# Five incidence rows of a graph layer turned by DMA, eleven by TensorE; the adjacency turned by DMA, its two halves added by GpSimd

## What is computed

```
L0: gt = adj.T;  x += (d^-.5 * gt * d^-.5) @ (h @ W0) + b0      d = row sums of gt
L1: mask = adj > 0;  inc = adj + mask / sqrt(row count of mask)
    x += (inc @ h) / row sums of inc
L2: ht = h @ W (4 heads of 256);  e = leaky_relu(src_i + dst_j) + adj
    x += mean over heads of softmax(e) @ ht
L3: x += relu(adj @ (binary(h) @ sign(W3).T))
```

## Time and profile before

| | |
|---|---|
| median of 3 runs | 754.05 us (753.78 to 754.13) |
| the profiled execution | 754.57 us, its span 752.8 us |
| PE busy | 731.1 us, 97% of the span |
| PE weight loads busy | 622.8 us, 83% |
| DVE busy | 648.9 us, 86% |
| ACT busy | 485.9 us, 65% |
| POOL busy | 62.6 us, 8% |
| DMA | 105.98 MB, mean 141 GB/s |
| mean granted TensorE clock | 0.984 |

### The profile page before, as it was taken

One profiled execution on the slowest core, in us unless ns is written; L12 is line 12 of the kernel. 1 busy time (PEld: TensorE's weight loads), 2 busy tenths in 40 slices (PEclk: granted clock), 3 DMA queues, 4 the chain that ended last, 5 costly groups with the idle time before them and its releaser, 6 DMA issues.

```text
span 752.8 us, 16841 instructions
## 1 busy us (share of the span) xinstructions
PE 731.1 (97%) x6816; PEld 622.8 (83%) x6816; DVE 648.9 (86%) x1196; ACT 485.9 (65%) x893; POOL 62.6 (8%) x102
## 2 busy tenths in 40 slices
PE   4999999999999999999999999999999999999998
PEld 3665888898889999546888888888888888888887
DVE  6788896868888886489999999999999999997683
ACT  4897020277677775587655877768696886766751
POOL 3004120211111110000000000000000000000000
PEclk7898999999999999999999999999999999999999
DMA  8886590055556633775011812135111713126691
GB/s 330 302 297 226 80 236 17 2 173 212 206 212 232 232 150 141 236 175 166 1 30 32 241 25 42 29 81 172 30 30 29 204 50 58 25 64 194 224 391 57
DMA packets 44173, 105.98 MB, mean 141 GB/s; under 512 B 3072, under 2 KB 17984, under 8 KB 39616
## 3 DMA queue, kind: packets, MB, share of 16 engines
q1 hardware_dynamic: 39824, 94.94, 36.4%
q0 software_dynamic: 4272, 9.96, 7.9%
HBM read 78.12 MB, written 18.91 MB: 129 GB/s over the span
## 4 chain that ended last, share of the span: by engine, by line
PE 83%; DVE 8%; ACT 6%; DMA 2%; issue 1%; SPq 0%; DVEq 0%; ACTq 0%
PE ps L746 15%; PE ps L747 15%; PE ps L748 15%; PE ps L686 4%; PE ps L788 3%; PE ps L789 3%; PE ps L582 3%; PE ps L581 3%; PE ps L580 3%; PE ps L609 3%; PE ps L633 2%; PE ps L635 2%; PE ps L634 2%; PE ps L613 2%; ACT arena L823 2%; DVE arena L1260 2%
## 5 line engine op out<-in xcount | busy, mean ns | idle before, releaser
L746 PE MATMUL ps<-arena 128*128 128x257 f16 x1024 | 280.0, 273 | 0.0
L748 PE MATMUL ps<-arena 128*128 128x257 f16 x1024 | 279.4, 273 | 0.0
L747 PE MATMUL ps<-arena 128*128 128x257 f16 x1024 | 279.3, 273 | 0.0
L1070 ACT ACTIVATE arena<-arena 128x512 f16<-128x512 f32 x252 | 158.5, 629 | 93.9 <-PE ps L748 61.9
L1393 DVE SCALAR_TENSOR_TENSOR arena<-arena,w_j 128x512 f32<-128x512 f32 x256 | 190.1, 744 | 0.0
L1400 DVE TENSOR_TENSOR arena<-arena 128x512 f16<-128x512 f32 x256 | 175.6, 687 | 3.7 <-ACT arena L1070 3.5
L747 PEld LDWEIGHTS ps<-arena 128*128 128x128 f16 x1024 | 100.3, 98 | 12.6
L748 PEld LDWEIGHTS ps<-arena 128*128 128x128 f16 x1024 | 99.8, 97 | 13.0
L746 PEld LDWEIGHTS ps<-arena 128*128 128x128 f16 x1024 | 99.9, 98 | 12.7
L633 PE MATMUL ps<-arena 128*128 128x257 f16 x256 | 70.3, 275 | 0.0
L635 PE MATMUL ps<-arena 128*128 128x257 f16 x256 | 69.7, 272 | 0.0
(11 more groups left out here) (154 smaller groups left out, 1183.8 us busy)
## 6 DMA issues: line engine op xcount, KB each, us to landing
arena<-in_adj_dram SPq DMA_DIRECT2D x32, 512.0 KB, 5.8
arena<-in_adj_dram SPq DMA_DIRECT2D x16, 1024.0 KB, 5.1
adj_t<-arena SPq DMA_DIRECT2D x16, 1024.0 KB, 5.5
arena<-adj_t SPq DMA_DIRECT2D x64, 256.0 KB, 4.1
arena<-adj_t SPq DMA_DIRECT2D x16, 1024.0 KB, 6.5
x<-arena POOLq DMA_DIRECT2D x15, 512.0 KB, 4.8
arena<-u_rows SPq DMA_DIRECT2D x4, 1024.0 KB, 13.6
x<-in_x_dram SPq DMA_DIRECT2D x4, 512.0 KB, 5.8
```

The costliest lines, as they stand in the source:

```text
L746: mm(ps[:, bank, 0:DE], hi, ht_hi[:, head, j, 0:DE], start=s, stop=False)
L747: mm(ps[:, bank, 0:DE], hi, ht_lo[:, head, j, 0:DE], start=False, stop=False)
L748: ins = mm(ps[:, bank, 0:DE], lo, ht_hi[:, head, j, 0:DE], start=False, stop=e)
L1070: nc.scalar.activation(p_hi[:, j % 4, :], prob[:, j % 4, :], copy).then_inc(p_hi_done, 1)
```

## The change

**Halves to DRAM.** Right after the loading stage SP writes all of `nat` (16 DMAs of 1 MB, in six lots with semaphores `nat_sent`) to a new DRAM tensor `adj_parts`. Whatever reuses that SBUF space waits for the lot.

**Layer 1.** Rows 0 to 4 (`AHEAD` = 5) are not turned by PE. In layer 0 ACT and DVE split `inc` of these rows as it lies (`inc_high`, `inc_low`, 2048 elements each), and SP turns both halves by DMA (`turn_inc`, two `dma_start_transpose` of 512 KB per row). Rows 5 to 15 are turned by PE, `inc` only, into three PSUM banks (`transpose_group`), and split by `part_high` (ACT) and `part_low` (DVE). The plain `adj` row is no longer turned by PE nor copied by ACT. The mask is made by ACT (`sign`, the Sign of the row, then `count` with Relu) and not by DVE. `w2_a` (16 small products on DVE) moves from layer 0 to t = 1 to 4 of layer 1, and `w2_lo` from t = 1 to 4 to t = 5 to 8. In layer 0 `maxima` is one block per t.

**`adj_t`.** It is now made in 16 tiles n = 4q + g (quarter q, columns group g). For each, SP turns the two halves from `adj_parts` (`turn_adj`, two `dma_start_transpose` of 512 KB), POOL adds them in four `tensor_tensor` of 128 x 512 f16 + f16 -> f32 (`widen`), and POOL issues one plain DMA of 1 MB to `adj_t`. The tiles 0 to 3 are widened in iterations 5 to 12 of layer 1, two instructions in each, tiles 4 and 5 before the first head is closed, and the others after the head closings of groups 0, 1, 2, 4 and 5, two tiles after each. `adj_t` now holds 256 times `adj`, and the exponential and the layer 3 split drop or add that factor.

**The rest.** The bias is added by POOL in the loading stage, 16 `tensor_tensor` of 128 x 256, in place of the four accumulating DMAs. The four `exp_adj` ahead of the attention weights move behind them: eight are made among `ht_high(5)` to `ht_high(12)`. The largest entry of `adj` is found at the end of layer 1 and no longer in layer 0. Rows 0 and 1 for layer 3 are split in heads 2 and 3 of the last quarter.

The core of the diff:

```diff
+            def turn_inc(t):
+                sp.wait_ge(inc_lo_done, t + 1)
+                for part in range(2):
+                    sp.dma_start_transpose(out=inc_parts[t % AHEAD][:, part, :, :], in_=inc_nat[t % 2][:, part, :]
+                                           ).then_inc(inc_in[t % AHEAD], 16)
+
+            def turn_adj(n):
+                q, g = n // TG, n % TG
+                if n >= 2:
+                    sp.wait_ge(widened, QB * (n - 1))
+                slot = (turn_l1 if q == 0 else turn_l2)[n % 2]
+                for part in range(2):
+                    sp.dma_start_transpose(out=slot[:, part, :, :],
+                                           in_=nat_dram[TG * P * g:TG * P * (g + 1), part, QB * P * q:QB * P * (q + 1)]
+                                           ).then_inc(turned[n % 2], 16)
...
+            for k, (lo, hi) in enumerate(SENT):
+                for b in range(lo, hi):
+                    sp.dma_start(nat_dram[b * P:(b + 1) * P], nat[:, b, :, :, :].rearrange("p a j n -> p a (j n)")
+                                 ).then_inc(nat_sent[k], 16)
...
             sp.wait_ge(ht_ps, 2 * NB)
-            for i in range(2):
-                sp.dma_start(adjt_early[i], adjt_dram[i]).then_inc(adjt_in[4 + i], 16)
+            for n in range(QB, 3 * QB):
+                turn_adj(n)
...
+            def widen(n, pieces=range(QB)):
+                buf = wide_l1 if n < QB else wide_l2
+                pool.wait_ge(turned[n % 2], 32 * (n // 2 + 1))
...
+                for r in pieces:
+                    nc.gpsimd.tensor_tensor(buf[:, r, :], turned_slot(n)[:, 0, r, :], turned_slot(n)[:, 1, r, :], ALU.add
+                                            ).then_inc(widened, 1)
+                if r == QB - 1:
+                    pool.wait_ge(widened, QB * (n + 1))
+                    nc.gpsimd.dma_start(wide_rows(n), buf).then_inc(wide[n % TG], 16)
...
             def transpose_group(t, g):
-                n = 4 * t + g
+                n = 4 * (t - AHEAD) + g
                 if g == 0:
-                    pe.wait_ge(rows_in[t % 4], 16 * (t // 4 + 1))
                     pe.wait_ge(filled, t + 1)
-                if n >= 2:
-                    pe.wait_ge(adjt_copied, n - 1)
-                    pe.wait_ge(inc_lo_done, n - 1)
+                if n < 3:
+                    pe.wait_ge(y_taken, NB)
+                else:
+                    pe.wait_ge(part_lo_done, n - 2)
...
+                if t >= AHEAD:
+                    pe.wait_ge(part_lo_done, 4 * (t - AHEAD) + g + 1)
+                elif g == 0:
+                    pe.wait_ge(inc_in[t], 32)
```

More of the change, by code:

```diff
@@ L410, in load_adjt @@
                              ).then_inc(adjt_in[k], 16)
-            for b in range(2):
-                sp.wait_ge(adjt_sent[b], 16 * NB // 2)
             for k in range(4):
@@ L500, in _ @@
                                     ).then_inc(head_added, 16)
+                for n in WIDEN_AFTER.get(group, ()):
+                    widen(n)
         @block.tensor
@@ L672, in _ @@
                         h2_transposes(t - 2)
-                    if g == 3 and t >= 2:
-                        if t == 2:
-                            pe.wait_ge(wa_done, 1)
+                    if g == 3 and t == 6:
+                        pe.wait_ge(wa_done, 1)
+                        for k in range(4):
+                            scores(k)
+                    if g == 3 and t >= 6:
                         scores(t - 2)
@@ L951, in _ @@
             h2_turned(NB - 1)
-            for j in range(4):
-                exp_adj(0, j)
             act.wait_ge(d_shift, 1)
@@ L977, in _ @@
             act.wait_ge(exps, 3)
+            for g in range(TG):
+                act.wait_ge(wide[g], 16)
             ht_high(0)
```

422 lines of the change are left out of this document (240 added, 182 removed).

## The result

The changed kernel takes 780.67 us (median of four: 777.51, 778.67, 782.67 and 795.02), the kernel before on the same chip 754.09 us. It is slower by 26.6 us. The ratio, 1.034 (95% interval 1.029 to 1.038), is taken without the 795.02, an execution in the slower state; without it the median is 778.67 and the kernel slower by 24.6 us. I had forecast 766, so the sign and the range held, and the size did not: +12 was forecast, about half of what came. The profiled execution is the lowest of them, 777.51 us with a span of 775.6, 22.8 us longer than the span of before.

What follows compares the result with a forecast made beforehand. The prediction took PE to bound layer 1, with PE and DVE both full in attention: 754.57 - 32 (layer 1) + 44 (attention) = 766.6, so 766 us; range 720 to 790, likeliest case 755 to 785.

Steps and rivals of the forecast that it cites:

- Part 2: Attention: POOL's 48 additions, 1.1 us each, hold DVE's two-input instructions in quarters 0 and 1; +44 us, bounds +9 to +102.
- spare time and lead: Attention, quarters 0 and 1: DVE's slack per group and its lead over PE absorb 8 to 9 us of holds.
- (a): Attention: POOL's reads don't hold DVE, so only layer 1's gain counts, 722 us; chance 0.20.
- (b): Attention: POOL's additions hold DVE only briefly, 0.36 to 0.7 us each, giving 738 us; chance 0.14.
- Part 1: Layer 1: 336 f32 transposes leave PE and the mask leaves DVE; -32 us, bounds -24 to -40.
- 5.3 + 32.8 + 32.8 + 23.1 + 22.8 = 117: Layer 1's length in us: iteration 0, then 1 to 4, 5 to 8, 9 to 11, and the last four.
- 1 us for the start: Start of layer 1: 1 us taken off the gain because row 0 must come through two turning DMAs.
- 7.25 plus 0.9 lost to POOL: Layer 1, iterations 5 to 8: DVE work of 7.25 us plus 0.9 held by POOL, 8.2 us per iteration.
- Part 3: What costs nothing: halves to DRAM, bias additions, ACT's mask, moved `exp_adj`, layer 3 rows, attention's turning DMAs and stores.
- 12 x 2 MB at the plain rate of 5.5 us per MB: Attention's 24 turning DMAs and 12 stores need 132 us of the DMA engines' available 260, so they fit.
- Rival (c): Layer 1 and attention: turning DMAs are slow, 19 us a pair and more, giving 780 to 810 us; chance 0.10.

Runs made afterwards that it cites:

- h_fill_order: Changed kernel with POOL's 64 additions replaced by fills that read nothing (adj_t left zero) and attention's turning DMAs issued later: 731.3 us.
- u_rows_first: `h_fill_order` with early maxima, fill of row 5 before low half of row 4, and loads of rows 6 to 8 before turning DMAs: 729.5 us.
- j_short_signs: Changed kernel, but for rows 3 to 5 of layer 1 ACT's sign takes 512 of 2048 columns and the count 128: 778.2 us.
- d_max_early: Changed kernel with the running maximum taking two blocks in each of layer 0's first eight iterations, none in the last eight: 777.5 us, ratio 1.032.
- m_fill_first: Changed kernel with converting/accumulating stores for additions, later turning DMAs, third tile slot with overlapped stores, row 5's fill before row 4's low half: 755.3 us, ratio 1.001.

## Why the prediction was right and wrong

**Part 2, right in its mechanism, and in its sum partly by luck.** The mechanism was forecast from one row, 0.9 us by which POOL waited for DVE, turned round by assumption. (The reading was a little loose: from 12.88 the DVE instruction had 1.05 us left and not 0.9, and POOL's reads there are not all of 1 to 4 elements, since the cast of the earlier trace rows reads 128, with nothing on DVE beside it.) The traces show it in both directions. The size was taken as 1.1 us from a cast of 128 x 128; it measures 1.19 in a row of four, 0.9 in turns, 1.0 on average. The stage is 45.1 us longer with 44 forecast, but two errors cancel there: 48 additions made 48.2 us of excess, where my sum had 4 x 8.8 + 2 x 8.8 = 53, and spare time and lead took some 3 us off it, where my sum took 9. Quarter 0 was to take 114 us in place of 85 and quarter 1 101 in place of 86. Counted from its first `numerators` to the next quarter's, which includes the four steps made early, they take 122.1 and 101.0 against 90.6 and 87.4 before, so 31.5 and 13.6 us more: 29 and 15 were forecast. Rivals (a) and (b) are out: `h_fill_order`, at 731.3, is what (a) would have looked like.

**Part 1, the step that failed: "5.3 + 32.8 + 32.8 + 23.1 + 22.8 = 117".** Of this sum its first terms failed: 5.3 for iteration 0 and 8.2 for iteration 1, with 1 us for the start. They took 14.8 and 11.3 after the end of layer 0, 11.5 us more. Everything behind them came out at 102.0 against 103.5. I counted what leaves PE and DVE inside layer 1, but not what the change puts into the end of layer 0: DVE splits and fills rows 0 to 4 there (2.3 us for each instruction), ACT signs, counts and splits them (1.9 us for each of the three), and the products with PE's last block of layer 0 wait on DVE behind all of it. "I take off 1 us for the start, where row 0 must have come through two turning DMAs" looked for the delay in the wrong place: PE began row 0's products right behind layer 0 and was stopped by `h1_low` and by the fill of row 5.

The experiments split it in part. Three reorderings together win back 4.1 of the 11.5 us (`u_rows_first`): the maxima 1.2, the order of fill and low half 1.1, the row loads behind turning DMAs 1.9, each from one profile against another. What `j_short_signs` took from ACT gave 3.5 on its own; how much of that is the same time as the 4.1 was not tried. About 2.3 us in the changed kernel are PE's clock at half after its idle time, which shrinks with that idle time, so they can't be added either. Some 7 us are left in `u_rows_first`. Its chain puts them on ACT; no run takes all of that work away, so this last part is argued.

**Iterations 5 to 12.** "7.25 plus 0.9 lost to POOL" four times is 3.6 us; from iteration 1 to 15 the kernel with fills takes 98.5, with additions 102.0: 3.5. The sum charged them to iterations 5 to 8 alone, though they stand in 5 to 12; the total came out all the same.

**Part 3, mostly right, with one hidden debt.** Loads, stores and the bias cost what was said: layer 0 starts 0.6 us later, within 0 to +3. But "12 x 2 MB at the plain rate of 5.5 us per MB are 132 us of the 260 that they have, so they fit" was too easy. A turning DMA of 512 KB from `adj_parts` costs the SP queue 3.4 us to issue (median; up to 8.4), and lands 7.2 us after its issue begins. Tiles come every 13 to 16 us through one buffer, and SP had the wrong ones first. That debt was invisible while the holds were there (0.4 us of waiting in the profiled execution) and 20 us once they were gone. The Trainium skill ("Advanced Engine Details and Errata", X-Bar Transpose) gives transposing DMAs on trn2 as being as fast as regular ones. For landing, this trace is not far from it: 7.2 us from DRAM, and 4.9 for the ten of layer 1 that read SBUF, where plain loads of 512 KB take 5.4 and 6.1; no run puts the two side by side under the same load. What the prediction left out was the time to issue them. Rival (c) was thus half right: not slow enough to set the time, slow enough to stand next in line.

**The median.** 3.2 us of the miss are the profiled execution's being the quickest (777.5 against 780.7; 1.2 against 778.67). Other executions of nearly the same program had a supply wait of 14 to 17 us ahead of quarter 1 with 6 to 8 us less of excess (`j_short_signs`, and the slowest one of `d_max_early`). Whether the slower executions of the changed kernel are of this kind is open, since they were not profiled.

## What to carry to other kernels

When work is moved out of a full stage, write down what the stage that receives it now does in its last few microseconds, engine by engine: the gain was forecast to 1.5 us where the work left, and was off by 11.5 where it arrived. An idle POOL is no free engine beside a DVE that reads two SBUF tensors without a pause: here its two-input instructions were added to DVE's time at 0.9 to 1.19 us for each 1.19 us of addition. And a limit that shows no wait may stand right behind the one that you see, so before building on its absence, take the first one away and look.

## What the runs showed of the hardware

- POOL's addition of 128 x 512 (f16 + f16 to f32) takes 1.19 us in a row of four, and such a row holds a two-input DVE instruction for all of it (5.51 in place of 0.74 us). Where the two engines take turns, each addition holds DVE by 0.9. A one-input copy of the same size takes 0.57 and holds the same way: 2.3 us for four in a row (2.98 in place of 0.69), 0.35 to 0.40 each in turns. A fill, which only writes, takes 0.48 and holds nothing (0.5 us of excess for 48).
- Sixteen plain stores of 1 MB issued within 21.5 us land 25.9 us (median) after their issue.
- A store that converts f16 to f32, or accumulates, takes 9.9 us for 1 MB written (`m_fill_first`), where a plain one takes 6.9, and with these stores the DMA share in quarter 0 is 1.16 and not 0.94. Taking the additions from POOL to the DMA engines was worth 21.0 us (772.4 to 751.4), of the 42.9 that fills give (729.5).
- A turning DMA of 512 KB from DRAM takes SP 3.4 us to issue (1.7 to 8.4), and what stands behind it in the same queue waits for that.
